# Layout of the scratch image planes and tokens in a four-layer image kernel on one Trainium2 core

## The chip, the cores and the metric

One core of a Trainium2 chip runs one launch of the whole program. The metric is the device time of that launch in microseconds (us). Everything is float32. The engines are PE (TensorE: matmuls and transposes), ACT (ScalarE), DVE (VectorE), POOL (GpSimd) and SP (SyncE, which here does nothing but issue DMAs and wait); 16 DMA engines move the data. Their mean busy share is called the DMA share below.

## The reference, cut to what matters

The input is an image of 256 x 256 pixels with 128 channels. Four layers follow one another, each a residual branch on a group-normed copy of the image: attention, a Fourier layer, a convolutional layer and a gated depthwise layer. The change touches the end of the third layer and the whole fourth:

```python
    # third layer, its last part: c2 is a matmul over channels at each pixel
    v = relu(c2(z)); p = concat([z[:, :, :1], z[:, :, 1:] + v[:, :, :-1]], axis=2)
    r = relu(c2(p)); q_main = r + roll(p, 1, axis=2)            # and the last two columns apart
    # fourth layer, T = 8 identical steps; the three 7x7 kernels are depthwise and circular
    gate_B = sigmoid(conv7x7(x, gate_B_kernel));  b_t = conv7x7(x, B_kernel) * gate_B
    a_t = A_kernel placed at the origin * sigmoid(conv7x7(x, gate_A_kernel))   # non-zero near the origin only
    log_h = heinsen_scan_log(...a_t, b_t, repeated T times...)
    out = x + exp(log_h[-1]) @ W_out + b_out
```

Away from the origin a_t is zero, so a pixel's result is a constant times (softplus(b_t) + 1e-6). A 7x7 patch at the origin is computed again in full at the end.

## The kernel before, in words

The stages run one after another, with a barrier of all engines between them. The last ones, in order, are `pointwise_part` (names begin with pw_), the group-norm coefficients, `patch_weights` (kw_), `depthwise_layer` (dw_) and `origin_patch` (og_). They pass data through three scratch tensors in DRAM.

`x3t[256 rows, 8 column offsets d, 32 patches, 128 ch]` is the third layer's result by tokens. `planes[33, 8 d, 8 y, 128 ch, 34]` is the same image by channels: the image is cut into patches of 8 x 8 pixels, and one cell (a channel's 34 numbers, 17,408 bytes for all channels) holds the pixels of one offset (y, d) of a row of patches, over all 32 patches and one wrapped patch on either side. Its rows are shifted by HALO = 3. `patch_w[32, 112, 2, 4, 128]` holds the depthwise taps spread into matmul weights.

`pointwise_part` steps over t, two image rows to a step, 128 steps plus 12 to drain. Per step SP loads two rows (L1374/L1376) and a broadcast row of tau (L1378) six steps ahead; DVE, PE, ACT and POOL pass them through z, v, p, r, q; DVE writes the result into `x3b` (L1520), which holds a band of 16 rows. Nine steps later PE turns the band's chunks (four patches each, eight chunks to a band) into `p_n` (L1450), and ACT copies each twice: into `x3n` (L1471), a double buffer that SP stores to x3t (L1389), and into `plane` (L1481). At the end of a band POOL fills the wrapped columns (L1423, L1424), and SP stores the whole band of `plane` at L1395 in three or four DMAs, one for each piece that `pieces(g)` finds. A piece is a run of n rows of one patch row; its DRAM side has the extents n x 8 x 4352, with n being 5, 8 and 3 in an inner band. SP's queue is in order, so the loads and token stores of the following steps stand behind these. ACT's L1471 waits at `tokens_stored` until the store of chunk e-2 has landed.

`patch_weights` makes 256 matmuls at 112 output rows (L1595) and stores patch_w in two DMAs (L1577).

`depthwise_layer` walks 8 blocks of 32 image rows. Its first half, per k (8 channels, 128 of them in all), loads windows (L1683, three DMAs: 24, 64 and 24 partitions, five patch rows, 1,080 bytes each) and twice 448 KB of weights (L1689), and PE does two `conv` (L1737, eight matmuls each, K = 112, the two halves being one patch row and the next). DVE and ACT copy the result into `raw`. Its second half, per unit u (128 of them), turns 8 pieces (L1749), ACT and DVE make gate, bt, soft and hid, PE projects (L1760), and DVE adds `xr`, the residual, into `outs` (L1880). The convs run 34 ahead (`lead`), so that k = u + 17. `xr` (L1695, 256 KB) is loaded in one DMA of 128 partitions, and `outs` is stored in four (L1702), one for each of four rows; the DRAM side of each has the extents 4 x 32 x 128, the SBUF side 128 x 128. All of it is issued by SP, which per unit does this:

```python
            for u in range(total + 8):
                k = u + lead // 2
                if k < BLOCKS * 16:
                    load_windows(k)      # waits for conv 2k-5
                    load_weights(2 * k)  # wait for conv 2k-4 and 2k-3
                    load_weights(2 * k + 1)
                if 0 <= u - 5 < total:
                    load_residual(u - 5)
                if 0 <= u - 8 < total:
                    store(u - 8)         # waits for added, then four DMAs
```

`origin_patch` loads a 13 x 13 patch of tokens in 27 short DMAs (L1943), and then computes the 49 pixels on one serial chain.

Of the kernel before, what the change touches and what calls it, by code (L numbers as in the profile page):

```python
# [1115 lines left out]
WIDE = PX + 2  # L1116
PATCH_ROWS = ROWS // PATCH + 1
# [183 lines left out]
def pointwise_part(nc, x2, tau, w2, b2, scale, shift, ident, x3t, planes, stats):  # L1301
# [6 lines left out]
    tokens = x3t.rearrange("(g y) d a c -> g (y d) (a c)", y=BAND)  # L1308
    with ExitStack() as ctx:
# [11 lines left out]
        x3b = m.sb("x3b", [128, 2, PX, BAND, PATCH])  # L1321
        x3n = m.sb("x3n", [128, 2, 4, CH])
# [8 lines left out]
        tokens_stored = [m.sem(f"tokens_stored{i}") for i in range(2)]  # L1331
# [3 lines left out]
        x3_made, counted, x3_turned = (m.sem(n) for n in ("x3_made", "counted", "x3_turned"))  # L1335
        tokens_read, plane_read, plane_wrapped = (m.sem(n) for n in ("tokens_read", "plane_read", "plane_wrapped"))
        block = ctx.enter_context(nc.Block())
        steps = range(-2, tiles + 12)

        def pieces(g):  # L1340

            first, found = g * BAND, []
            runs = [(y, min(y + BAND, ROWS), HALO) for y in (first,)]
            if g == 0:
                runs.append((0, PATCH - HALO, HALO + ROWS))
            if g == ROWS // BAND - 1:
                runs.append((ROWS - HALO, ROWS, HALO - ROWS))
            for start, stop, offset in runs:
                while start < stop:
                    at = start + offset  # L1350
                    n = min(stop - start, PATCH - at % PATCH)
                    found.append((start - first, n, at // PATCH, at % PATCH))
                    start += n
            return found

        def plane_stores(parity, g):

            return 16 * sum(len(pieces(k)) for k in range(parity, g, 2))

        @block.sync  # L1360
        def _(sp):
# [21 lines left out]
            for t in steps:  # L1383
# [3 lines left out]
                if 0 <= e < chunks:  # L1387
                    sp.wait_ge(tokens_read, e + 1)
                    sp.dma_start(tokens[e // 8][:, e % 8 * 4 * CH:(e % 8 + 1) * 4 * CH],  # L1389
                                 x3n[:, e % 2].rearrange("p a c -> p (a c)")).then_inc(tokens_stored[e % 2], 16)  # L1390
# [236 lines left out]
def depthwise_layer(nc, x3t, planes, patch_w, ksum, scale, shift, w_plain, b_plain, ident, out):  # L1627
# [11 lines left out]
    with ExitStack() as ctx:  # L1639
# [145 lines left out]
        def _(act):  # L1785
# [34 lines left out]
            for u in range(total + 2):  # L1820
# [3 lines left out]
                if 2 <= u:  # L1824
                    soft_first(u - 2)
# [345 lines left out]
```

## Time and profile before

| | |
|---|---|
| median of 3 runs | 7585.48 us (7583.73 to 7593.19) |
| the profiled execution's own time, and its span | 7594.39 us, 7592.7 us |
| mean granted TensorE clock over the span | 0.904 of full speed |
| PE, DVE, ACT, POOL busy | 6234.0 (82%), 3902.4 (51%), 3821.1 (50%), 569.5 us (8%) |
| moved by DMA | 773.64 MB, 102 GB/s over the span |
| matmuls of conv (L1737) | 643.6 us busy for x4096, and 412.5 us idle before them |
| ACT's first gate step (L1795) | 99.4 us busy, 792.2 us idle before it |

The page cuts the span in 40 slices of 190 us. Its rows of tenths show the busy share of each engine, of the DMA engines, and the clock that TensorE was granted:

```profile
PE   7999999999999999977999899854444557777763
PEclk9999999999999999999999999987777568888886
DMA  5111111111111111673111111355444189888882
```

Up to slice 26 attention and the Fourier layer run; `pointwise_part` fills slices 27 to 31, `patch_weights` the end of 31 and 32, and `depthwise_layer` the rest but for the last 66 us. SPq is SP's queue: its durations are the time that issuing the DMAs took. A matmul in float32 leaves two records, and its records overlap in time.

### The profile page before, as it was taken

What the parts mean: (1) busy time and instruction counts of PE and PEld (TensorE: products, weight loads), DVE (VectorE), ACT (ScalarE), POOL (GpSimd) and SP (SyncE); (2) the same over time, 40 slices, a digit from 0 to 9 for tenths busy, and PEclk for the clock granted to TensorE, in tenths of its full rate; (3) what the DMA queues carried; (4) which work ended last, traced back from release to release, by engine and by line L of the source; (5) the groups of instructions that cost most, each with busy time, mean ns of one, the idle gap of its engine ahead of it and who ended that gap; (6) DMA issues with size and microseconds to landing.
All of it is one profiled execution on the core that took longest, in us unless ns stands there. A gap on an engine that the chain in (4) does not pass through costs nothing. (4 is left out here: it accounts for less than half of the span.)

```text
span 7592.7 us, 110044 instructions
## 1 busy us (share of the span) xinstructions
PE 6234.0 (82%) x29856; PEld 4091.6 (54%) x29856; DVE 3902.4 (51%) x11300; ACT 3821.1 (50%) x9727; POOL 569.5 (8%) x879
## 2 busy tenths in 40 slices
PE   7999999999999999977999899854444557777763
PEld 5777777777777776424444344311111347766663
DVE  7777777777777777413333333224444203333335
ACT  3777777777777776223444444433333203333333
POOL 0000000000000000001000000013333000111111
PEclk9999999999999999999999999987777568888886
DMA  5111111111111111673111111355444189888882
GB/s 200 34 35 35 35 34 35 35 34 34 35 35 35 34 35 41 211 230 96 59 61 56 62 59 61 107 187 164 161 156 157 52 204 207 196 195 199 196 197 70
DMA packets 759166, 773.64 MB, mean 102 GB/s; under 512 B 52640, under 2 KB 631769, under 8 KB 748121
## 3 DMA queue, kind: packets, MB, share of 16 engines
q1 hardware_dynamic: 738986, 719.10, 33.9%
q0 software_dynamic: 13312, 41.96, 1.4%
q10 hardware_dynamic: 6720, 10.76, 0.4%
q8 instruction: 75, 1.23, 0.1%
q14 instruction: 73, 0.60, 0.0%
HBM read 566.01 MB, written 205.61 MB: 102 GB/s over the span
## 5 line engine op out<-in xcount | busy, mean ns | idle before, releaser
L428 ACT ACTIVATE at_probs<-at_neg_s,at_neg_max 128x256 f32<-128x256 f32 x2048 | 1018.0, 499 | 327.1 <-DVE at_neg_max L480 320.6
L359 PE MATMUL at_p_s<-at_keys,at_qz 128*128 128x256 f32 x4096 | 1107.0, 393 | 3.2 <-ACT at_qz L453 2.5
L480 DVE CUSTOM_DVE_ANT_0 at_neg_s<-at_p_s,at_bias 128x256 f32<-128x256 f32 x2048 | 782.2, 419 | 592.7 <-PE at_p_s L359 592.6
L1737 PE MATMUL dw_p_conv<-dw_xw,dw_wts 112*128 112x128 f32 x4096 | 643.6, 323 | 412.5 <-issue 349.1
L1737 PEld LDWEIGHTS dw_p_conv<-dw_xw,dw_wts 112*128 112x128 f32 x4096 | 609.8, 235 | 433.7 <-issue 432.9
L359 PEld LDWEIGHTS at_p_s<-at_keys,at_qz 128*128 128x128 f32 x4096 | 697.7, 190 | 267.4 <-issue 209.1
L347 PE MATMUL at_p_o<-at_probs_t,at_vs 128*32 128x256 f32 x4096 | 810.0, 385 | 0.0
L492 DVE TENSOR_SCALAR at_probs<-at_probs,at_inv 128x256 f32<-128x256 f32 x2048 | 631.0, 351 | 36.2
L339 PE MATMUL at_p_t<-all_ident,at_probs 128*128 128x128 f32 x4096 | 587.1, 276 | 1.6 <-DVE at_probs_t L471 1.6
L1443 PE MATMUL pw_p_r<-pw_p,pw_w 128*128 128x512 f32 x256 | 170.4, 753 | 459.8 <-DVE pw_p L1498 459.6
L339 PEld LDWEIGHTS at_p_t<-all_ident,at_probs 128*128 128x128 f32 x4096 | 466.8, 141 | 133.1 <-issue 105.9
L1795 ACT ACTIVATE dw_gate<-dw_p_turn,dw_f_shift,dw_nscale 128x512 f32<-128x512 f32 x128 | 99.4, 777 | 792.2 <-PE dw_p_turn L1749 792.2
L935 PE MATMUL ml_p<-ml_h,l_w 128*128 128x512 f32 x1024 | 485.0, 597 | 1.6 <-DVE ml_h L1002 1.6
L347 PEld LDWEIGHTS at_p_o<-at_probs_t,at_vs 128*32 128x32 f32 x4096 | 284.7, 109 | 368.2 <-issue 128.2
L951 PE MATMUL ml_p<-ml_h,l_w1s 128*128 128x512 f32 x1024 | 469.2, 601 | 1.3 <-DVE ml_normed L1010 1.3
L1872 DVE SCALAR_TENSOR_TENSOR dw_hid<-dw_bt,dw_soft 128x512 f32<-128x512 f32 x128 | 135.2, 1057 | 592.5 <-ACT dw_soft L1813 592.5
L422 ACT ACTIVATE at_probs_t<-at_p_t 128x512 f32<-128x512 f32 x512 | 305.9, 597 | 249.6 <-PE at_p_t L339 243.3
L453 ACT ACTIVATE at_qz<-at_p_qk 32x256 f32<-32x256 f32 x1024 | 384.3, 375 | 92.0 <-PE at_p_qk L405 82.9
L981 ACT ACTIVATE ml_h<-ml_p,l_b 128x512 f32<-128x512 f32 x384 | 248.0, 679 | 282.6 <-PE ml_p L935 282.6
L428 ACT ACTIVATION_READ_ACCUMULATOR at_probs<-at_neg_s,at_neg_max 128x1 f32 x2048 | 386.2, 189 | 0.0
L1443 PEld LDWEIGHTS pw_p_r<-pw_p,pw_w 128*128 128x128 f32 x256 | 49.0, 226 | 567.5 <-DVE pw_p L1498 547.0
L471 DVE COPY at_probs_t<-at_p_t 128x512 f32<-128x512 f32 x512 | 349.3, 682 | 0.5 <-PE at_p_t L339 0.5
(214 smaller groups left out, 9837.9 us busy)
## 6 DMA issues: line engine op xcount, KB each, us to landing
dw_wts<-patch_w SPq DMA_DIRECT2D x256, 448.0 KB, 8.2
sp_xs<-x SPq DMA_DIRECT2D x256, 256.0 KB, 3.2
dw_xw<-planes SPq DMA_DIRECT2D x128, 337.5 KB
in_xs<-in_x_dram SPq DMA_DIRECT2D x32, 1024.0 KB
at_xs<-in_x_dram SPq DMA_DIRECT2D x256, 128.0 KB, 2.1
at_kvs<-in_L_conv_kv_x_dram SPq DMA_DIRECT2D x256, 128.0 KB, 2.3
x<-at_x1s SPq DMA_DIRECT2D x256, 128.0 KB, 1.9
ml_xs<-x SPq DMA_DIRECT2D x128, 256.0 KB
```

The costliest lines, as they stand in the source:

```text
L339: mm = pe.transpose(p_t[h % 2][:, kh, qh * 128:(qh + 1) * 128], probs[:, h, qh, kh * 128:(kh + 1) * 128], ident[:, :])
L347: mm = pe.matmul(p_o[ch, 0, :], vs[:, row.r % 2, kh, ch], probs_t[:, h, kh, :], start=kh == 0, stop=kh == HALVES - 1)
L359: mm = pe.matmul(p_s[h % 2][:, qh, :], qz[:, row.r % 2, h, qh * 128:(qh + 1) * 128], keys[:, row.r, h // 2, :], start=True, stop=True)
L422: act.activation(probs_t[:, h], p_t[h % 2][:, :, :], ACT.Copy).then_inc(odd_read, 1)
L428: e = act.activation(probs[:, h, qh, :], neg_s[:, h % 2, qh, :], ACT.Exp, bias=neg_max[:, row.r % 2, i:i + 1], scale=-1.0, accum_out=sums[ ...
L453: t = act.activation(qz[ch, two.r % 2, h, :], p_qk[ch, 0, :], ACT.Copy, scale=float(HEAD_DIM) ** -0.5)
L471: dve.tensor_copy(probs_t[:, h], p_t[h % 2][:, :, :]).then_inc(even_read, 1)
L480: t = dve.tensor_tensor_reduce(neg_s[:, h % 2, qh, :], p_s[h % 2][:, qh, :], bias[:, h, qh, :], -1.0, 3.0e38, ALU.add, ALU.min, neg_max[:, ...
L492: t = dve.tensor_scalar(probs[:, h, qh, :], probs[:, h, qh, :], inv[:, p, j:j + 1], None, ALU.mult)
L935: pe.matmul(p_1[b][:, :], w0[:, b * 128:(b + 1) * 128], h[:, :], start=True, stop=True).then_inc(hid_made, 1)
L951: mm = pe.matmul(p_2[:, :], w1c[:, b, :], h1[:, b, :], start=b == 0, stop=b == blocks - 1)
L1737: mm = pe.matmul(p_conv[g % 2][:, j, :], wts[:, g % 4, half, j, :], xw[:, k % 3, half:half + BLOCK_PY, g % 2 * 4 + j, 0:PX], start=half == ...
```

## The change

The cells of `planes` become 16 rows x 8 columns on 128 partitions. A cell row is now an image row of 8 offsets, `planes[264, 8, 128 ch, 33]`, with the image shifted by SHIFT = 4 rows, and with 4 wrapped rows above and below. A conv window lies in two horizontally neighbouring cells, so that the two halves of a conv are the cell and the one to its right; a window load is one DMA of 128 partitions x 4 patch rows x 1,056 bytes. The weights take 128 rows rather than 112.

`x3t` becomes `[16 bands, 33 cells, 129, 128 ch]`. The tokens are shifted by 4 columns, and the 33rd cell wraps. `x3b` has 33 cells too; each DVE instruction of L1520 becomes two of half the size, and POOL copies the wrapped half cell once a band. PE and DVE wait for that.

The stores of `plane` go out in eight parts of 2,112 bytes on 128 partitions, one in each of the eight steps after the band, and the steps go on 20 beyond the last, not 12. POOL fills one wrapped column, not two. `x3n` has four buffers, and its stores are now pieces of 512 bytes rather than 2,048; every eighth step has one more, of 64 KB.

In `depthwise_layer` the residual comes in four DMAs of 32 partitions, one step later, and the result leaves in four of 32 partitions, x 4 rows x 512 bytes. ACT issues those at the end of its step, for unit u - 9, instead of SP. `xr` and `outs` have four buffers. `origin_patch` cuts its pieces at the cell edges too: about 53 loads rather than 27.

```diff
@@ pointwise_part
-        x3n = m.sb("x3n", [128, 2, 4, CH])
+        x3n = m.sb("x3n", [128, 4, 4, CH])
+        part = CH * WIDE // 8
@@ SP
-                if e >= 0 and e % 8 == 7:
-                    g = e // 8
-                    sp.wait_ge(plane_wrapped, g + 1)
-                    for y, n, r_at, y_at in pieces(g):
-                        sp.dma_start(planes[r_at, :, y_at:y_at + n].rearrange("d y c a -> y d (c a)"),
-                                     plane[y * PATCH:(y + n) * PATCH, g % 2].rearrange("p c a -> p (c a)")
-                                     ).then_inc(planes_stored[g % 2], 16)
+                f = t - 18
+                if 0 <= f < chunks:
+                    g, k = f // 8, f % 8
+                    flat = plane[:, g % 2].rearrange("p c a -> p (c a)")
+                    if k == 0:
+                        sp.wait_ge(plane_wrapped, g + 1)
+                    sp.dma_start(body[g][:, k * part:(k + 1) * part], flat[:, k * part:(k + 1) * part]
+                                 ).then_inc(planes_stored[g % 2], 16)
@@ PE, and the same for DVE's bn_stats
                     pe.wait_ge(x3_made, 8 * g + 8)
+                    pe.wait_ge(x3_wrapped, g + 1)
@@ DVE
                     for i in range(2):
-                        x3 = dve.scalar_tensor_tensor(out=x3b[:, g % 2, :, y + i, :],
+                        for d, a_at in ((0, 1), (SHIFT, 0)):
+                            cols = slice(SHIFT - d, 2 * SHIFT - d)
+                            x3 = dve.scalar_tensor_tensor(
+                                out=x3b[:, g % 2, a_at:a_at + PX, y + i, d:d + SHIFT],
@@ depthwise_layer
-        xw = m.sb("xw", [WROWS, 3, BLOCK_PY + 1, 8, WIDE])
+        xw = m.sb("xw", [128, 3, BLOCK_PY, 8, WIDE])
@@ SP
-                for d, n, at, col in ((PATCH - HALO, HALO, 0, 0), (0, PATCH, HALO, 1), (0, HALO, HALO + PATCH, 2)):
-                    sp.dma_start(flat[at * PATCH:(at + n) * PATCH, k % 3, :, 0:run],
-                                 field(b * BLOCK_PY, d, 0, c, col, n)).then_inc(x_loaded[k % 3], 16)
+                sp.dma_start(flat[:, k % 3], windows(b, c)).then_inc(x_loaded[k % 3], 16)
...
-            def store(w):
-                r, x, y = w // 4, w // 2 % 2 * 4, w % 2 * 4
-                sp.wait_ge(added, w + 1)
-                for i in range(4):
-                    sp.dma_start(out[0, r * PATCH + y + i].rearrange("(a d) c -> d a c", d=PATCH)[x:x + 4],
-                                 outs[:, w % 3, i]).then_inc(stored[w % 3], 16)
+                for d in range(4):
+                    sp.dma_start(xr[d * PX:(d + 1) * PX, w % 4], cells[(1 - x) * SHIFT + d][:, y:y + 4]).then_inc(r_loaded[w % 4], 16)
@@ PE
-                        mm = pe.matmul(p_conv[g % 2][:, j, :], wts[:, g % 4, half, j, :],
-                                       xw[:, k % 3, half:half + BLOCK_PY, g % 2 * 4 + j, 0:PX],
+                        mm = pe.matmul(p_conv[g % 2][:, j, :], wts[:, g % 4, side, j, :],
+                                       xw[:, k % 3, :, g % 2 * 4 + j, side:side + PX], start=side == 0, stop=side == 1)
@@ ACT
+            def store(w):
+                r, x, y = w // 4, w // 2 % 2 * 4, w % 2 * 4
+                act.wait_ge(added, w + 1)
+                for d in range(4):
+                    act.dma_start(out[0, r * PATCH + y:r * PATCH + y + 4].rearrange("y (a d) c -> d a y c", d=PATCH)[x + d],
+                                  outs[d * PX:(d + 1) * PX, w % 4]).then_inc(stored[w % 4], 16)
...
                 if u < total:
                     gate_third(u)
+                if 9 <= u:
+                    store(u - 9)
@@ origin_patch
-                k = min(left, 128 - at % 128)
+                k = min(left, 128 - at % 128, PATCH - (x + SHIFT) % PATCH)
```

## Rows read from the trace of the kernel before

**Rows 1.** SP's queue: start us, duration us; band stores of the pointwise stage and its end.
```profile
5154.59 6.18 SPq L1395 DMA_DIRECT2D planes<-pw_plane  x4
...
5214.35 3.78 SPq L1395 DMA_DIRECT2D planes<-pw_plane  x3
...
5944.77 6.01 SPq L1395 DMA_DIRECT2D planes<-pw_plane  x4
5981.09 0.35 SPq L1570 DMA_DIRECT2D all_taps<-in_L_conv_B_kernel_dram  x1
```

**Rows 2.** SP's queue around one band store, 5595 to 5624 us.
```profile
5595.83 3.77 SPq L1395 DMA_DIRECT2D planes<-pw_plane  x3
...
5612.19 3.14 SPq L1378 DMA_DIRECT2D pw_taus<-tau  x1
5623.70 0.32 SPq L1389 DMA_DIRECT2D x3t<-pw_x3n  x1
```

**Rows 3.** Who waited for whom, 5200 to 5700 us: total us, times, longest.
```profile
ACT pw_x3n L1471 <- DMA x3t<-pw_x3n: 224.6, 9, 25.2
```

**Rows 4.** Stretches: length, busy of PE, PEld, DVE, ACT, POOL; clock, DMA share, GB/s.
```profile
5122.00:5150.00 28.00, 20.18 (x63) 9.01 (x63) 23.37 (x36) 17.09 (x31) 17.07 (x31) 0.94 0.69 216
5560.00:5569.00 9.00, 0.00 (x0) 0.00 (x0) 0.00 (x0) 0.00 (x0) 0.00 (x0) 0.50 0.26 93
6112.00:6150.00 38.00, 0.00 (x0) 0.00 (x0) 0.00 (x0) 0.00 (x0) 0.00 (x0) 0.50 0.86 285
6200.00:6260.00 60.00, 43.43 (x271) 41.91 (x270) 6.08 (x9) 5.38 (x9) 0.00 (x0) 0.76 1.03 221
6400.00:7300.00 900.00, 640.37 (x4138) 626.50 (x4139) 306.94 (x431) 296.77 (x520) 110.03 (x86) 0.83 0.85 197
7404.00:7500.00 96.00, 63.45 (x334) 61.57 (x335) 57.72 (x75) 52.75 (x90) 24.60 (x19) 0.71 0.36 104
```

**Rows 5.** Groups by line, 5122 to 5150 us: shapes xcount | busy us, mean ns | idle before.
```profile
L1520 DVE SCALAR_TENSOR_TENSOR pw_x3b<-pw_xs,all_coef,pw_q 128x256 f32<-128x256 f32 x14 | 6.2, 481 | 4.5 <-POOL pw_q L1418 4.3
```

**Rows 6.** DVE in order of time: two instructions of L1511, eight steps apart.
```profile
5121.77 1.67 DVE L1511 SCALAR_TENSOR_TENSOR pw_z<-pw_xs,all_coef,pw_taus 128x512 f32<-128x512 f32 x1
...
5152.85 0.74 DVE L1511 SCALAR_TENSOR_TENSOR pw_z<-pw_xs,all_coef,pw_taus 128x512 f32<-128x512 f32 x1
```

**Rows 7.** SP's queue: first window load, the 18th and the last of 128.
```profile
6154.36 1.66 SPq L1683 DMA_DIRECT2D dw_xw<-planes  x3
...
6266.93 1.65 SPq L1683 DMA_DIRECT2D dw_xw<-planes  x3
...
7394.44 1.98 SPq L1683 DMA_DIRECT2D dw_xw<-planes  x3
```

**Rows 8.** SP's queue in one unit of the depthwise stage.
```profile
6804.65 0.38 SPq L1695 DMA_DIRECT2D dw_xr<-x3t  x1
6805.07 5.52 SPq L1702 DMA_DIRECT2D out_dram<-dw_outs  x4
6810.64 1.90 SPq L1683 DMA_DIRECT2D dw_xw<-planes  x3
6812.59 0.83 SPq L1689 DMA_DIRECT2D dw_wts<-patch_w  x2
```

**Rows 9.** PE in order of time through one unit.
```profile
6809.72 2.02 PE L1737 MATMUL dw_p_conv<-dw_xw,dw_wts 112*128 112x128 f32 x16 [2.04 <-issue]
6811.58 1.05 PE L1760 MATMUL dw_p_out<-all_w_plain,dw_hid 128*128 128x128 f32 x8
6812.47 1.96 PE L1737 MATMUL dw_p_conv<-dw_xw,dw_wts 112*128 112x128 f32 x16
6814.26 1.33 PE L1749 MATMUL dw_p_turn<-all_ident,dw_raw 128*128 128x128 f32 x8
```

**Rows 10.** ACT's queue, a store of the Fourier layer.
```profile
3211.72 0.32 ACTq L641 DMA_DIRECT2D spec<-sp_out  x1
```
**Rows 11.** SP's queue, the loads of the origin patch.
```profile
7527.34 9.02 SPq L1943 DMA_DIRECT2D og_xs<-x3t  x27
```

More of the change, by code:

```diff
@@ L1330, in pointwise_part @@
         wrap_loaded = m.sem("wrap_loaded")
-        tokens_stored = [m.sem(f"tokens_stored{i}") for i in range(2)]
+        tokens_stored = [m.sem(f"tokens_stored{i}") for i in range(4)]
         planes_stored = [m.sem(f"planes_stored{i}") for i in range(2)]
@@ L1334, in pointwise_part, with token_stores @@
         r_mul, r_made, p_wrapped, q_made = (m.sem(n) for n in ("r_mul", "r_made", "p_wrapped", "q_made"))
-        x3_made, counted, x3_turned = (m.sem(n) for n in ("x3_made", "counted", "x3_turned"))
+        x3_made, x3_wrapped, counted, x3_turned = (m.sem(n) for n in ("x3_made", "x3_wrapped", "counted", "x3_turned"))
         tokens_read, plane_read, plane_wrapped = (m.sem(n) for n in ("tokens_read", "plane_read", "plane_wrapped"))
         block = ctx.enter_context(nc.Block())
[L1338 to L1354, printed above, removed]
+        steps = range(-2, tiles + 20)
+        bands = ROWS // BAND
+        edge = SHIFT * PATCH
+        first_row = planes[0:SHIFT].rearrange("y d c a -> (y d) (c a)")
+        last_row = planes[ROWS + SHIFT:ROWS + 2 * SHIFT].rearrange("y d c a -> (y d) (c a)")
+        body = planes[SHIFT:ROWS + SHIFT].rearrange("(g y) d c a -> g (y d) (c a)", y=BAND)
+        part = CH * WIDE // 8
+        def token_stores(e):
+            return 16 * (e // 4) + (16 * len(range(0, e, 8)) if e % 4 == 0 else 0)
         def plane_stores(parity, g):
-            return 16 * sum(len(pieces(k)) for k in range(parity, g, 2))
+            return 16 * 8 * len(range(parity, g, 2)) + (16 if parity == 0 and g > 0 else 0) + (16 if g == bands and parity else 0)
         @block.sync
@@ L1559, in patch_weights @@
         p_t = m.ps("p_t", [KTAPS, 2, CH])
-        p_w = [m.ps(f"p_w{i}", [WROWS, 2, 2, CH]) for i in range(4)]
+        p_w = [m.ps(f"p_w{i}", [128, 2, 2, CH]) for i in range(4)]
         p_b = m.ps("p_b", [128, CH])
@@ L1658, in depthwise_layer @@
         w_loaded = [m.sem(f"w_loaded{i}") for i in range(4)]
-        r_loaded = [m.sem(f"r_loaded{i}") for i in range(3)]
-        stored = [m.sem(f"stored{i}") for i in range(3)]
+        r_loaded = [m.sem(f"r_loaded{i}") for i in range(4)]
+        stored = [m.sem(f"stored{i}") for i in range(4)]
         scaled, prepared, biased = m.sem("scaled"), m.sem("prepared"), m.sem("biased")
@@ L1712, in _ @@
                 load_weights(2 * k + 1)
-            for u in range(total + 8):
+            for u in range(total + 6):
                 k = u + lead // 2
@@ L1718, in _ @@
                     load_weights(2 * k + 1)
-                if 0 <= u - 5 < total:
-                    load_residual(u - 5)
-                if 0 <= u - 8 < total:
-                    store(u - 8)
-            for s in range(3):
-                sp.wait_ge(stored[s], 64 * ((total - s + 2) // 3))
+                if 0 <= u - 6 < total:
+                    load_residual(u - 6)
         @block.tensor
@@ L1833, in _ @@
                     gate_third(u)
+                if 9 <= u:
+                    store(u - 9)
+            for s in range(4):
+                act.wait_ge(stored[s], 64 * (total // 4))
         @block.gpsimd
@@ L1877, in residual @@
                 dve.wait_ge(biased, w + 1)
[L1878 to L1880 removed]
+                if w >= 4:
+                    dve.wait_ge(stored[w % 4], 64 * (w // 4))
+                dve.tensor_tensor(outs[:, w % 4], p_out[w % 2][:, :, :], xr[:, w % 4], ALU.add).then_inc(added, 1)
             for g in range(0, lead, 2):
@@ L1937, in origin_patch, with cells @@
         loads = len(pieces) + 4 + 2 * SIDE
+        def cells(y, x, k):
+            first = y % BAND * PATCH + x % PATCH
+            return x3t[y // BAND, x // PATCH, first:first + k]
         @block.sync
```

114 lines of the change are left out of this document (58 added, 56 removed).

## The prediction

> **What bounds the kernel now.** Only the last 2500 us or so are touched, so I read the page's slices first and then go by stages. In slices 27 to 31 and from 33 on PE is not full, and the DMA share is either low (4 or 5 tenths) or high (8). These are two different limits.
>
> *The pointwise stage.* The stores of a band go out at 5154.59, 5214.35 and so on, the last of 16 at 5944.77, and the next stage begins at 5981.09 [rows 1]. The 15 bands between take 790 us, 52.7 each, or 6.6 us a step. But the first band, when no planes are yet being stored, runs at 31.08 us for eight steps, 3.89 each [rows 6]. So nearly half of the stage is something else. SP's queue shows it: the band's store is issued at 5595.83, everything behind it takes 1 to 3 us to issue, and the next token store gets out at 5623.70 only [rows 2]. ACT stands at L1471 for a token store to land, 224.6 us in 500, 25 us at a time [rows 3]. What is in flight then is seen in the stretches: at 5560 to 5569 no engine works, and the 16 DMA engines are 0.26 busy at 93 GB/s [rows 4]. A share of 0.26 over engines that have work queued means that about 4 of 16 do it. The stores of plane are cut along an outer extent of 5, 8 and 3, and those of patch_w, whose outer extent is 112, reach 0.86 at 285 GB/s [rows 4]. I read this as: a store is spread over as many engines as its outer extent allows.
>
> The Trainium skill, "DMA: Bandwidth & Descriptors", section on why a DMA increments its semaphore by 16, says that a copy runs on the largest number up to 16 that divides both sides' slowest extents. By it 5, 8 and 3 engines work for plane, a mean of 4 to 5 of 16, and the share of 0.26 agrees; it also gives 4 for the result's stores, below.
>
> *The depthwise stage.* 110 units pass between the 18th window load at 6266.93 and the last at 7394.44: 10.25 us each [rows 7]. PE needs about 6.36 us of them (2.02 + 1.05 + 1.96 + 1.33) and waits before conv for nothing an engine did ("issue"), that is, for a load [rows 9]. DVE and ACT work 307 and 297 us in 900, or 86 units: 3.6 and 3.4 us a unit [rows 4]. The DMA share is 0.85 at 197 GB/s. But SP has no idle time: the four result stores take 5.52 us to issue, windows 1.90, weights 0.83, the residual 0.38 [rows 8]. One residual load carries as much as all four stores and takes a fourteenth of the time to issue, so the stores are held back by full queues, on the few engines that they reach, and the loads that PE waits for stand behind them.
>
> **What the DMA engines can do.** I divide GB/s by share in each stretch of [rows 4]: 216/0.69 = 313 in the pointwise stage's clean band, 285/0.86 = 331 for patch_w, 104/0.36 = 289 in the depthwise tail (512-byte pieces only); but 221/1.03 = 215 in the depthwise lead (windows and weights on 112 partitions, no stores), and 197/0.85 = 232 in its steady part. That the lead is so slow at 4,096- and 1,080-byte pieces is the open point: either it is the uneven 24-, 64- and 24-partition loads and the 112 rows, which go, or the source layout, which stays. Bounds for the new stage: 232 and 331.
>
> **The change part by part.**
> 1. *Plane stores in eight even parts.* The stall goes. What is late next is the step's own loop: 3.89 us [rows 6]. L1520 becomes four instructions of half the size. One of 256 elements takes 481 ns [rows 5]; one of 128 takes between half of that and all of it, so a step gains 0 to 0.96 us. With a fixed part of about 0.2 us I take 0.25: 4.13 a step. POOL's wrap is one small copy a band and the waits on it fall a step before they are needed: nothing; were it late, a POOL copy is under 0.7 us a band (10 us in all). From the first band store, moved to 5159, 110 steps to the last image step come to 454 us (5613), the ten drain steps to about 2 us each (5633). The end, now 36 us, shrinks: 2.2 MB at 93 GB/s take 24 us, at 313 GB/s 7, so 19 are left. End at 5652 instead of 5981: 329 gained. ACT's wait for the plane buffer at a band's first chunk now comes in the same step in which the last part is issued; up to 2 us a band, of which I count 9 in all. **−320** (bounds −230, all of 0.96 a step, and −350). The DMA load of a step is four transfers of about 262 KB, 1.07 MB in 4.13 us, 260 GB/s, which is under 313: near the limit, but not at it.
> 2. *patch_w* grows from 14.7 to 16.8 MB; its store runs at 285 GB/s: 0 to +7, **+4**.
> 3. *Lead of the depthwise stage.* 17 k in 112.6 us, 6.62 each [rows 7]. Now 541 KB of windows and 1,049 of weights (before 605 and 918). At 313 GB/s 5.1 us, which is above the two convs' 4.0: **−26** (at 215: +13).
> 4. *A unit of the steady part.* Bytes: 541 + 1,049 + 262 of residual + 262 of result = 2,114 KB, 3% more than before. Windows and weights at 313 give 5.1 us, the 512-byte transfers at 289 1.8, together 6.9. PE needs 6.36, SP now 0.6 + 0.83 + 4 x 0.4 = 3.0, ACT 3.4 + 4 x 0.4 (issues of 0.32 [rows 10] with gaps) = 5.1 in busy time. Nothing has slack to spare, so 6.9 won't be met wholly: **7.2 us**, 110 x (10.25 − 7.2) = **−336**. Bounds: PE's 6.4 (−423) and 2,114 KB at 232 GB/s, 9.1 (−127). I take the fast side because 313, 289 and 331 are three stretches with evenly spread transfers, and 215 and 232 the two without.
> 5. *ACT's stores.* Behind them on ACT stands the next gate step, which PE's turns two units on and, through DVE's copy, the next conv wait for. They wait for `added` of unit u − 9, which DVE made two steps before: no wait. The tail of 17 units (7404 to 7500: ACT 52.75 of 96 busy [rows 4]) may lose what the issues cost ACT, and gains SP's: nothing. The last stores spread: **−5**.
> 6. *Origin patch.* 27 loads take 9.02 us to issue [rows 11]; 26 more at 0.334 on the serial path: **+9**.
>
> Sum: −320 + 4 − 26 − 336 − 5 + 9 = −674. From the profiled execution's 7594.4: 6920; it lies 8.9 above the median of the runs, so **6910** for the median.
>
> **The rivals.**
> - *A faster case* is inside the forecast's own range: 6.4 us a unit gives 6820.
> - *B. The rate stays.* The loads run at 215 to 232 because of the cells' pitch in DRAM or of the mixture. Then a unit is 9.2 us and the lead 7.4: 6910 + 220 + 39 = 7170. For it: the share of 1.03 in the lead with no store in sight [rows 4]. Against it: the clean stretches.
> - *C. 32 partitions.* Residual and result now touch 32 partitions at a time. If that halves the tail's rate, to 145 GB/s, they cost 3.6 us instead of 1.8, and a unit about 8.8: +176, 7085. The tail, with 128 partitions, cannot show it. The Trainium skill, "SBUF — State Buffer", section on the DMA port swizzle, says that partitions 0 to 31 reach 8 of 16 ports, 189 GB/s at 1 MiB; by it the two cost an estimated 2.8 us, and the sum would be 110 higher. No row here tests it.
> - *D. The jam moves to ACT.* If the four stores still take 5.5 us to issue, ACT needs 3.9 (its six instructions end to end) + 5.5 = 9.4 a unit: 7150. The skill's DMA page, "Issuing engines are not separate DMA queues", says that another issuer saves its own issue time only; that the present hold-up lies in few engines speaks against D.
> - *E. The pointwise stall stays,* because the parts are not spread as I think, or because 512-byte token stores replace it by a DMA limit: some 260 of the 320 are lost, 7170.
> - *F. Slower than before.* D with a worse price: ACT's issues block so long that the gate chain runs late each unit. It decides from 674/110 + 7.2 = 13.3 us a unit, that is 9.4 us for four issues, against 5.52 now; at 11 us a unit takes 14.9 and the time is 7760.
>
> **How the numbers follow.** Chances: forecast 0.58, B 0.14, C 0.12, D 0.08, E 0.06, F 0.02. The forecast's own range, from its bounds without B's rate, is 6790 to 7030. Eight in ten reach from 6780 to 7180, which takes in B to D as priced. A difference of under 0.2% could not be told from none. All but F are faster by far more: faster 0.97, within 0.2% 0.01, slower 0.02.
>
> **What would show it.** Pointwise: band stores about 33 us apart, ACT's wait for token stores gone, DMA share 0.7 to 0.85, and the stage's end about 320 us earlier. If bands take 38 us or more, DVE's four instructions or the DMA rate were mis-sized. Depthwise: window loads 7.2 us apart, GB/s around 290 in the steady part, SP idle for over half, the 512-byte stores on ACT's queue 1.3 to 1.7 us a group, PE's granted clock up from 0.83 as it waits less. B would show as a share near 1 at under 235 GB/s, in the lead too; C as a normal lead and a slow steady part; D as store groups over 4 us on ACT's queue.

## The result: 6768 us, and the profile after

The changed kernel takes 6768.24 us (median of 4 runs, 6760.24 to 6776.89); its ratio to the kernel before is 0.892 (95% interval 0.8904 to 0.8935). The kernel before, with a fourth run, has a median of 7588.18 us. That is faster by 820 us, where 674 were forecast, and 12 us below the lower end of the range. The profiled execution has a span of 6766.9 us against 7592.7.

The stages can be cut at the same instructions of SP's queue in both traces: the first load of each stage, the 18th window load, the last window load.

| stage | before, us | after, us | change | forecast |
|---|---|---|---|---|
| up to the pointwise stage | 5077.3 | 5078.1 | +0.8 | 0 |
| pointwise, with the coefficients | 903.8 | 557.3 | −346.4 | −320 |
| patch_weights | 173.3 | 165.0 | −8.2 | +4 |
| depthwise, lead (17 k) | 112.6 | 70.5 | −42.0 | −26 |
| depthwise, 110 units | 1127.5 | 704.5 | −423.0 | −336 |
| depthwise, tail | 132.9 | 118.6 | −14.3 | −5 |
| origin patch | 65.4 | 72.9 | +7.5 | +9 |

The cuts are rows like these, of SP's queue in the changed kernel (start us, duration us); they answer to [rows 1, 7 and 11]:

```profile
5635.42 0.34 SPq L1577 DMA_DIRECT2D all_taps<-in_L_conv_B_kernel_dram  x1
...
5800.45 0.36 SPq L1688 DMA_DIRECT2D dw_xw<-planes  x1
...
5870.98 0.93 SPq L1688 DMA_DIRECT2D dw_xw<-planes  x1
...
6575.46 0.44 SPq L1688 DMA_DIRECT2D dw_xw<-planes  x1
...
6694.03 16.40 SPq L1952 DMA_DIRECT2D og_xs<-x3t  x53
```

The same kernel's stretches, with the columns of [rows 4] (length, busy of PE, PEld, DVE, ACT and POOL, granted clock, DMA share, GB/s): the pointwise stage after its first bands, the store of patch_w, the lead, the steady part and the tail.

```profile
5157.00:5558.00 401.00, 277.51 (x794) 121.08 (x793) 357.31 (x696) 228.06 (x397) 232.38 (x425) 0.92 0.90 270
5765.00:5795.00 30.00, 0.00 (x0) 0.00 (x0) 0.00 (x0) 0.00 (x0) 0.00 (x0) 0.50 1.03 386
5815.00:5865.00 50.00, 45.32 (x385) 43.54 (x384) 8.15 (x13) 7.17 (x12) 0.00 (x0) 1.00 1.03 377
5950.00:6500.00 550.00, 500.36 (x4087) 486.39 (x4087) 297.09 (x424) 291.86 (x510) 114.79 (x85) 1.00 1.09 328
6600.00:6670.00 70.00, 44.89 (x245) 42.16 (x243) 47.36 (x60) 43.58 (x74) 21.07 (x15) 0.78 0.43 115
```

Three things are to be seen beside [rows 4]. In the steady part PE is 91% busy at a granted clock of 1.00 (before: 71% at 0.83), the DMA engines move 328 GB/s instead of 197, and they are full (share 1.09; it sums the times of packets and passes 1 where these overlap). In the lead, with no store in sight in either kernel, the rate went from 221 to 377 GB/s at the same share of 1.03. And in the pointwise stage DVE is busy 357 of 401 us.

One number from such a row is used for every run below. A unit leaves 48 matmul records (32 of conv, 8 of turn, 8 of project), so a stretch's length over its PE count, times 48, is the time of a unit: 550/4087 x 48 = 6.46 us here, 900/4138 x 48 = 10.44 us in [rows 4]. (The table's 704.5/110 gives 6.40, since the first units are quicker.)

PE's order of time through one unit in the changed kernel, as in [rows 9]:

```profile
6304.15 2.02 PE L1731 MATMUL dw_p_conv<-dw_xw,dw_wts 128*128 128x128 f32 x16 [0.69 <-issue]
6306.01 1.06 PE L1753 MATMUL dw_p_out<-all_w_plain,dw_hid 128*128 128x128 f32 x8
6306.91 1.95 PE L1731 MATMUL dw_p_conv<-dw_xw,dw_wts 128*128 128x128 f32 x16
6308.69 1.33 PE L1742 MATMUL dw_p_turn<-all_ident,dw_raw 128*128 128x128 f32 x8
6310.65 2.02 PE L1731 MATMUL dw_p_conv<-dw_xw,dw_wts 128*128 128x128 f32 x16 [0.62 <-issue]
```

From 6304.15 to 6310.65 is 6.50 us. The four groups add up to 6.36, but their records overlap at the joints, so that PE works 5.88 and waits 0.62, before the first conv only. The 6.36 that the prediction took as PE's least was too much by this overlap.

### The profile page after: what moved, and what is told of

Its sections match the earlier page's. It is cut to its first block and busy times, and to the rows that moved or that the text cites. A ratio compares the mean times of both kernels' runs of the same rounds, so it can differ in the third digit from the quotient of the medians.

```text
span 6766.9 us, 110680 instructions
## 1 busy us (share of the span) xinstructions
PE 6039.0 (89%) x29856; PEld 3899.9 (58%) x29856; DVE 3958.6 (58%) x11556; ACT 3822.8 (56%) x9727; POOL 587.2 (9%) x879
## 5 line engine op out<-in xcount | busy, mean ns | idle before, releaser
L1731 PE MATMUL dw_p_conv<-dw_xw,dw_wts 128*128 128x128 f32 x4096 | 509.5, 277 | 122.5 <-issue 64.3
L1731 PEld LDWEIGHTS dw_p_conv<-dw_xw,dw_wts 128*128 128x128 f32 x4096 | 479.7, 190 | 142.7 <-issue 141.0
L935 PEld LDWEIGHTS ml_p<-ml_h,l_w 128*128 128x128 f32 x1024 | 195.7, 191 | 250.7 <-issue 246.0
L1010 DVE SCALAR_TENSOR_TENSOR ml_normed<-ml_p,l_vec,ml_rstd 128x512 f32<-128x512 f32 x128 | 96.1, 751 | 410.6 <-ACT ml_rstd L975 410.6
L707 POOL DMA_DIRECT2D mixed<-mx_gs x64 | 34.8, 545 | 3350.3 <-DVE mx_gs L767 3345.8
```

The source lines that it names most:

```text
L935: pe.matmul(p_1[b][:, :], w0[:, b * 128:(b + 1) * 128], h[:, :], start=True, stop=True).then_inc(hid_made, 1)
L1731: mm = pe.matmul(p_conv[g % 2][:, j, :], wts[:, g % 4, side, j, :], xw[:, k % 3, :, g % 2 * 4 + j, side:side + PX], start=side == 0, stop= ...
```

## The experiments

Theory 1 is the prediction's: how a transfer is cut decides how fast it drains, and SP's queue passes a slow one's price on to all that stands behind it. Theory 2, its main rival, is the other half of the change: what counts is that loads and stores shared one queue. A third question came with the result: why loads alone, in the lead, are 1.7 times as fast. Times are of one run where no interval is given; they are compared with 7588 (before) and 6768 (after).

### The result's stores: their cut and their queue

Four runs cross the two halves. In the kernel before, the even cut alone:

```diff
-                for i in range(4):
-                    sp.dma_start(out[0, r * PATCH + y + i].rearrange("(a d) c -> d a c", d=PATCH)[x:x + 4],
-                                 outs[:, w % 3, i]).then_inc(stored[w % 3], 16)
+                for d in range(4):
+                    sp.dma_start(out[0, r * PATCH + y:r * PATCH + y + 4].rearrange("y (a d) c -> d a y c", d=PATCH)[x + d],
+                                 outs[d * PX:(d + 1) * PX, w % 3]).then_inc(stored[w % 3], 16)
```

> The kernel before, with one edit: the result's four stores of a unit are cut as in the changed kernel (32 partitions x 4 rows of 512 bytes each, DRAM side 32 x 4 x 128), still issued by SP from the same place; the data and the bytes are the same. Theory 1 (a store reaches only as many DMA engines as its outer extents allow, and the old cut reached few): the group of four issues falls from 5.5 us to about 2, PE's next limit is the rate of windows and weights, 1522 KB at 221 GB/s plus 524 KB at 289 GB/s = 8.7 us a unit instead of 10.25, total about 7415 us (7380 to 7480). Theory 2 (what matters is that SP's queue issues loads and stores in turn, whatever their cut): the unit stays at 10.25 us and the total at 7588, within 20.

Measured: 7409.4 us, theory 1's number (7415) and far from theory 2's. A unit takes 800/4387 x 48 = 8.75 us, as the sum of bytes over rates had given (8.7). The new limit is plain in the steady stretch of this run: the DMA share is 1.02 at only 235 GB/s, against 0.85 and 197 in [rows 4].

```profile
6400.00:7200.00 800.00, 624.52 (x4387) 610.78 (x4388) 334.88 (x458) 313.74 (x550) 124.40 (x92) 0.88 1.02 235
```

Then ACT's queue alone, with the old cut:

```diff
-                if 0 <= u - 8 < total:
-                    store(u - 8)         # SP
+                if 9 <= u:
+                    store(u - 9)         # ACT, after gate_third(u)
```

> The kernel before, with one edit: the result's stores keep their old cut (four DMAs of 128 partitions, DRAM side 4 x 32 x 128) but ACT issues them, for unit u-9, and SP's queue has loads alone. Theory 1: the few engines that carry the stores stay the slowest, so the hold-up moves to ACT's queue (groups of about 5 us there) and a unit stays at 9.5 us or more, total 7500 to 7650. Theory 2: SP's queue is free, a unit falls to 7 or 8 us, total 7250 to 7350.

Measured: 7495.6 us, 4 us below theory 1's range and 145 above theory 2's; a unit takes 800/4064 x 48 = 9.45 us. The hold-up is now on ACT's queue, and the next gate step (L1785) waits behind it:

```profile
6810.59 0.55 ACTq L1812 DMA_DIRECT2D out_dram<-dw_outs  x1
6810.93 0.62 ACT L1803 ACTIVATE dw_soft<-dw_soft 128x512 f32<-128x512 f32 x1
6811.45 0.71 ACT L1794 ACTIVATE dw_gate<-dw_gate,dw_log_scale 128x512 f32<-128x512 f32 x1
6811.46 6.65 ACTq L1812 DMA_DIRECT2D out_dram<-dw_outs  x3
6818.25 0.78 ACT L1785 ACTIVATE dw_gate<-dw_p_turn,dw_f_shift,dw_nscale 128x512 f32<-128x512 f32 x1 [6.09 <-PE dw_p_turn L1739]
```

This is the prediction's rival D, made to happen. It shows that the queue is worth something too: 93 us while the cut is uneven. In the changed kernel the old cut was put back, ACT still issuing (the first diff in reverse):

> The changed kernel, with one part undone: the result's stores are cut as before (four DMAs of 128 partitions, DRAM side 4 x 32 x 128, one image row each), but ACT still issues them; which partitions hold which pixels is the same in both cuts, so the result is too. Theory 1: the engines that they reach carry 66 KB more than the others, a unit rises from 6.5 to 8 us or more, total 6930 or more. Theory 2: the cut doesn't matter, total 6768 within 20.

Measured: 6982.8 us, 215 more; a unit takes 550/3099 x 48 = 8.52 us, at a DMA share of 0.90 and 248 GB/s. Theory 1 again, which had asked for 8 us or more and 6930 or more. Last, the new cut, issued by SP again:

```diff
+                if 0 <= u - 8 < total:
+                    store(u - 8)         # SP, behind load_residual(u - 6)
-                if 9 <= u:
-                    store(u - 9)         # ACT
```

> The changed kernel, with one part undone: the result's stores, in their new even cut, are issued by SP again, for unit u-8 behind the residual's loads. Theory 1: SP needs 0.5 + 1 + 1.9 + 1.7 = 5 us of the 6.5 us of a unit, nothing is late, total within 30 us of the changed kernel's 6768. Theory 2: loads wait behind stores again, at least 1 us a unit, total 6880 or more.

Measured: 6859.5 us (ratio to before 0.9035, 0.902 to 0.905), 91 more than the changed kernel. Both expectations missed: mine of at most 30, and theory 2's of 112 or more. SP had time enough to issue (its four stores take 1.76 us). It was the wait in front of them, in this run's list of who waited for whom from 5950 to 6500 us:

```profile
SPq L1715 <- DVE dw_outs L1884: 100.1, 59, 3.8
```

SP's loads run two units ahead of PE, and `store(u - 8)` makes it wait for a sum that DVE has yet to make. If so, an older unit's store waits for nothing:

```diff
-                if 0 <= u - 8 < total:
-                    store(u - 8)
+                if 0 <= u - 10 < total:
+                    store(u - 10)
```

> The changed kernel with the stores of the result issued by SP in the even cut, as in the run that lost 91 us, but two units later (u-10 instead of u-8). In that run SP waited at the store for DVE's sum, 100 us in 550, with the next loads behind it. If that wait is what ACT's queue saves, it is gone here, and the total is 6768 within 15. If the issuing itself costs (SP's queue shared by loads and stores), at least 40 us of the 91 stay.

Measured: 6756.1 us (ratio 0.8905, 0.8891 to 0.8919), all of the 91 us back and 12 more. A unit takes 450/3362 x 48 = 6.42 us. So ACT's queue as such gives nothing: it spares SP a wait, and so does a store two units later. Whether the 12 us beyond are real is taken up below.

### Why loads alone became faster

Each load of weights in the changed kernel was split in two, first at partition 112 and then at 64 as its control:

```diff
-                sp.dma_start(wts[:, g % 4], patch_w[g % groups]).then_inc(w_loaded[g % 4], 16)
+                for lo, hi in ((0, 112), (112, 128)):      # in the other run (0, 64), (64, 128)
+                    sp.dma_start(wts[lo:hi, g % 4], patch_w[g % groups][lo:hi]).then_inc(w_loaded[g % 4], 16)
```

> The changed kernel, with one edit: each load of weights is two DMAs, of partitions 0 to 111 and 112 to 127; bytes are the same. It asks why the lead of the depthwise stage runs at 370 GB/s where it ran at 221 before. If loads onto 112 partitions are slow by themselves, most of the difference comes back: lead under 290 GB/s, a unit of the steady part over 7 us, total over 6830. If it was the three uneven window loads or the source's layout, nothing comes back but for the issues: total under 6800.

> The changed kernel, with one edit: each load of weights is two DMAs of 64 partitions. The control for the 112-partition edit: two DMAs as there, but on even numbers of rows per engine. If the 112 are the cause there, this one is nearer to the changed kernel (370 GB/s in the lead, total under 6800), unless half the partitions at a time are slower by themselves; if two DMAs instead of one are the cause, both lose alike.

Measured: 6992.8 and 6989.4 us, and units of 8.05 and 8.31 us. The lead's rate, in the stretch of 377 GB/s above, in the run at 112 and the run at 64:

```profile
5815.00:5865.00 50.00, 30.74 (x231) 28.88 (x231) 4.84 (x7) 4.78 (x8) 0.00 (x0) 0.95 1.07 251
```

```profile
5815.00:5865.00 50.00, 31.29 (x239) 29.03 (x238) 5.53 (x8) 4.18 (x7) 0.00 (x0) 0.97 1.07 249
```

The same bytes, the same share, two thirds of the rate. But both lose alike, so it isn't the odd number 112. Either any load that doesn't span the 128 partitions is slow, or two DMAs are. The same split in two along the free side tells:

```diff
+                for side in range(2):
+                    sp.dma_start(wts[:, g % 4, side], patch_w[g % groups][:, side]).then_inc(w_loaded[g % 4], 16)
```

> The changed kernel, with one edit: each load of weights is two DMAs of all 128 partitions, 2,048 bytes each (the two sides apart). The control that the runs with 112 + 16 and 64 + 64 partitions left open: they fell from 377 to about 250 GB/s in the lead alike. If that was because no DMA of theirs spans the 128 partitions, this one stays near the changed kernel: lead over 340 GB/s, total under 6810. If it was because there are twice as many DMAs, this one falls as they did: lead near 250 GB/s, total about 6990.

Measured: 6769.7 us, a lead at 359 GB/s, a unit of 450/3288 x 48 = 6.57 us. As many DMAs as in the two runs before, and nothing is lost in the total. So what costs is the cut along the partitions, and not the number of DMAs.

The Trainium skill, "SBUF — State Buffer", section on the DMA port swizzle, says that only a transfer over all 128 partitions reaches all 16 ports at once and that 0 to 63 reach no more than 0 to 31; the run at 64 agrees (249 GB/s against 377 and 359). The run at 112 is as slow (251), and there the port count explains less: by the same section's table, 0 to 111 touch all 16 ports, unevenly. Whether its part of 112 or its rest of 16 partitions is the slow one was not tried.

From the other side: the kernel before with 16 rows of zeros added to the weights.

```diff
-    patch_w = scratch("patch_w", [CH // 4, WROWS, 2, 4, 2 * SPOTS])
+    patch_w = scratch("patch_w", [CH // 4, 128, 2, 4, 2 * SPOTS])
-        wts = m.sb("wts", [WROWS, 4, 2, 4, 2 * SPOTS])
+        wts = m.sb("wts", [128, 4, 2, 4, 2 * SPOTS])
```

> The kernel before, with one edit: the scratch weights have 128 rows, of which the last 16 are zeros, and the weights' loads and the store of patch_w span the 128 partitions; the convs still use 112 rows. If the span of 128 partitions is what makes loads fast, weights land faster though they have 14% more bytes: the lead's rate rises from 221 GB/s, at least to 270, and its 18 window loads take under 100 us instead of 113. The steady part is held by the stores on few engines and stays near 10.25 us a unit; total 7540 to 7590. If the layout of the source is the cause, the lead gets longer by the bytes, 118 us or more.

Measured: 7494.6 us, 94 less than before, for 14% more bytes of weights. The store of patch_w, whose partitions are the one thing about it that changed, now runs at the changed kernel's rate; before, it had a share of 0.86 and 285 GB/s [rows 4]:

```profile
6115.00:6145.00 30.00, 0.00 (x0) 0.00 (x0) 0.00 (x0) 0.00 (x0) 0.00 (x0) 0.50 1.03 384
```

The lead did not follow. From its first window load (6159.92) to the 18th (6272.23) it takes 112.3 us, against 112.6 before: neither the 100 of the one explanation nor the 118 of the other. Its rate from 6200 to 6250 us is 218 GB/s. So whole weights alone don't make the lead fast. What this lead lacks against the changed kernel's 70.5 us lies with the windows, the only load in it that still differs: three DMAs of 24, 64 and 24 partitions and five patch rows became one of 128 partitions and four. An estimate from these runs: at 377 GB/s the 1,049 KB of weights take 2.8 of this run's 6.6 us a k, and the rest leaves 158 GB/s for 605 KB of windows. Whether the windows were slow by their cut or by their layout in DRAM no run separates. The steady part, which I had expected unchanged, went to 800/4162 x 48 = 9.23 us a unit. Why it gained what the lead didn't is open.

### What sets a unit of 6.5 us now

The rest is PE's 5.88 us of work and 0.62 of waiting. Half of the weights' bytes were left out, with all waits kept:

```diff
-                sp.dma_start(wts[:, g % 4], patch_w[g % groups]).then_inc(w_loaded[g % 4], 16)
+                sides = slice(0, 2) if g < 4 else slice(0, 1)
+                sp.dma_start(wts[:, g % 4, sides], patch_w[g % groups][:, sides]).then_inc(w_loaded[g % 4], 16)
```

> The changed kernel, leaving out a part: from the fifth group on only the weights of one side are loaded, 256 KB instead of 512 KB; the convs use old data for the other side. PE's work and every wait are as before. It asks what sets the 6.50 us of a unit, in which PE works 5.88 and waits 0.62 before the first conv. If it is the DMA engines (share 1.09), a unit falls to 5.9 us, total about 6700. If it is the chain of turn, gates, copy and conv over ACT and DVE, or the granted clock, the unit stays at 6.5 and the total within 15 of 6768, but for the lead.

Measured: 6675.3 us, and PE has no gap left in its groups by line from 5950 to 6400 us (shapes xcount | busy us, mean ns | idle before):

```profile
L1732 PE MATMUL dw_p_conv<-dw_xw,dw_wts 128*128 128x128 f32 x2529 | 311.3, 274 | 0.0
L1743 PE MATMUL dw_p_turn<-all_ident,dw_raw 128*128 128x128 f32 x639 | 106.8, 310 | 0.0
L1754 PE MATMUL dw_p_out<-all_w_plain,dw_hid 128*128 128x128 f32 x632 | 83.8, 276 | 0.0
```

A unit takes 450/3800 x 48 = 5.68 us. With fewer bytes the DMA engines' hold on the unit is gone and PE is busy throughout. So the changed kernel's units are bound by the DMA engines, as the prediction said, at 328 GB/s, and PE is only 0.8 us behind.

### The plane stores

In the kernel before, a band's stores were issued row by row:

```diff
-                        sp.dma_start(planes[r_at, :, y_at:y_at + n].rearrange("d y c a -> y d (c a)"),
-                                     plane[y * PATCH:(y + n) * PATCH, g % 2].rearrange("p c a -> p (c a)")
+                        for i in range(n):
+                            sp.dma_start(planes[r_at, :, y_at + i].rearrange("d c a -> d (c a)"),
+                                         plane[(y + i) * PATCH:(y + i + 1) * PATCH, g % 2].rearrange("p c a -> p (c a)")
```

> The kernel before, with one edit: the stores of a band of plane go out one image row at a time (16 or more DMAs of 8 partitions x 17,408 bytes) instead of in pieces of 5, 8 and 3 rows; the bytes are the same, and so is the place in SP's queue. If a store is spread by its outer extent, each now reaches 8 engines instead of 5, 8 and 3: the 2.2 MB drain in about half the time, the DMA share in the stall is near 0.5 instead of 0.26, and the band's period falls from 54 us to 42 to 46 (stage 120 to 190 us shorter, total about 7430). Rival (the stall is the write rate of these long pieces in DRAM, or their place in the queue): period 54 us as before, total 7588 within 20.

Measured: 7597.8 us. The time is the rival's, and of the theory only the share came true. In the stall, where the kernel before had a share of 0.26 and 93 GB/s [rows 4]:

```profile
5560.00:5569.00 9.00, 0.00 (x0) 0.00 (x0) 0.00 (x0) 0.00 (x0) 0.00 (x0) 0.57 0.50 114
```

Twice the share, and a quarter more bytes a second; SP takes 19.83 us to issue the band's 16 DMAs. More engines are not the remedy by themselves. Why they moved so little each, this run doesn't show. The opposite edit in the changed kernel kept the old pieces, which there have one merged extent:

```diff
-                    sp.dma_start(body[g][:, k * part:(k + 1) * part], flat[:, k * part:(k + 1) * part]
-                                 ).then_inc(planes_stored[g % 2], 16)
+                        for lo, hi in ((0, 40), (40, 104), (104, 128)):   # all at k == 0
+                            sp.dma_start(body[g][lo:hi], flat[lo:hi]).then_inc(planes_stored[g % 2], 16)
```

> The changed kernel, with one edit: a band of plane goes out in three DMAs of 40, 64 and 24 partitions x 16,896 bytes, the pieces of the kernel before, but with (row, offset) as one outer extent of 40, 64 and 24, since the new cells lie in that order. If the old extents of 5, 8 and 3 were the cause, these are spread over 8 engines or more, and the stage is within 60 us of the changed kernel's 557. If a store has to span the 128 partitions to be fast, the drain stays near 120 GB/s, ACT waits for token stores at each band again, and the stage is 200 us longer or more (about 760 or more).

Measured: 6782.1 us; the stage, from its first load at 5079.89 to the next stage's at 5653.04, takes 573 us against 557. ACT's waits for a token store, 224.6 us in 500 before [rows 3], come to this in 401 us:

```profile
ACT pw_x3n L1476 <- DMA x3t<-pw_x3n: 26.0, 12, 4.4
```

In the changed kernel there is no such wait in this stretch. While the three pieces of a band drain, with the step's other transfers, the engines move nearly three times what they did in the stall before:

```profile
5421.00:5431.00 10.00, 5.64 (x17) 2.46 (x18) 9.70 (x18) 5.57 (x10) 6.90 (x11) 1.00 0.84 273
```

So the stores of plane need not span the 128 partitions, nor be cut in eight: three whole pieces do nearly as well in the new layout. What in it does this is not separated. The outer extent is now 40, 64 or 24 and not 5, 8 or 3; but a piece is now also one unbroken run in DRAM, where two neighbouring offsets of a row used to lie 139 KB apart, and x3n has four buffers instead of two. And all eight parts at once:

```diff
-                    sp.dma_start(body[g][:, k * part:(k + 1) * part], flat[:, k * part:(k + 1) * part]
+                        for h in range(8):                                # all at k == 0
+                            sp.dma_start(body[g][:, h * part:(h + 1) * part], flat[:, h * part:(h + 1) * part]
```

> The changed kernel, with one part undone: the eight even parts of a band of plane are all issued in one step, not one a step. If the gain in the pointwise stage is from the even cut, the burst of 2.2 MB takes 7 us at over 300 GB/s, of which loads six steps ahead hide nearly all: the stage is within 30 us of the changed kernel's 557, total under 6800. If it is from the spreading over time, ACT and the loads stall at each band again by 5 us or more: stage 80 us longer, total 6850.

Measured: 6777.5 us, the stage 551 us (5083.16 to 5634.51). Spreading the parts over the steps gives nothing that one run can show.

### A version that beats both

The price of the new layout is 26 more short loads in the last stage. They can be shared with ACT:

```diff
-            for at, y, x, k in pieces:
+            for at, y, x, k in pieces[0::2]:          # SP; ACT issues pieces[1::2] and the residual's 14
```

> The changed kernel, with one edit: in the last stage half of the 53 token loads and all 14 loads of the residual are issued by ACT, which is idle there, while SP issues the rest. The 16.4 us of SP's issues become about 8.5, and the residual's 4.4 run beside them: total 8 to 13 us less, 6757. If the last loads' landing or ACT's table load behind the issues sets the end instead, less than 5 us.

Measured: 6755.2 us (ratio 0.8902, 0.889 to 0.8914). The stage takes 63.3 us instead of 72.9. Both queues run side by side:

```profile
6698.66 8.45 SPq L1952 DMA_DIRECT2D og_xs<-x3t  x27
6698.67 8.25 ACTq L1981 DMA_DIRECT2D og_xs<-x3t  x26
```

With the late stores from SP, and beside the changed kernel itself on the same chip:

> The changed kernel with two edits that were run alone: the result's stores issued by SP two units late, and the last stage's short loads shared between SP and ACT. They touch different stages, so the gains should add: 12 and 13 us below the changed kernel's 6768, that is 6743 (6735 to 6752). If the 12 us of the late stores are the difference between chips, 6755.

> The changed kernel itself, unedited, on the chip of the version above, to compare the two at equal terms. 6768 within 10.

Measured: 6751.2 us (6742.66 to 6755.77; ratio to before 0.8893, 0.888 to 0.8905) against 6771.3 (6758.99 to 6773.35; 0.8919, 0.8906 to 0.8932). It is 20 us, or 0.3%, faster than the changed kernel; of these the last stage gives 9.7 (72.8 to 63.1 us in the two traces) and the depthwise stage 5.1 (895.9 to 890.8). The two edits gave less together than the 25 expected. Which of them was worth less than it seemed is open: the runs of each edit alone and these two sets all come from one chip, so it was not a difference between chips, and the runs of one kernel lie up to 17 us apart.

## Why the prediction was wrong, point by point

**What bounds the kernel** was right in both stages: b_even_stores came within 6 us of a number worked out from it, and the pointwise stall went with the new stores. The reading that a store is spread over as many engines as its outer extent allows is borne out in the share (0.50 for an extent of 8), though loosely in the stall itself: 5, 8 and 3 have a mean of 5.3 engines, a share of 0.33, where 0.26 was seen. But the prediction took it for the whole cause of the slow drain, and b_row_stores shows that it isn't: the share doubled and the time stayed. What else the new layout does for these stores is open.

**The step that failed is "What the DMA engines can do".** It set 331 GB/s at full share as the upper bound, from the store of patch_w. That store itself ran on 112 partitions, and so was slowed by the very thing that the change removes: on 128 it runs at 386 GB/s, share 1.03, and at 384 in the kernel before with nothing but the 16 rows added (b_w128). The lead runs at 377, not 313. The text named the uneven loads and the 112 rows as one of two explanations of the slow 215 and took the fast side, but then priced it from the stretches of before, none of which had whole-partition loads of 4,096 bytes in it. (b_w128 shows that the weights' 112 rows alone were not what held the lead; the windows remain.) Every term on that rate was too small:
- the lead: 4.1 us a k instead of 5.1, −42 instead of −26;
- patch_weights: −8 instead of +4, at 14% more bytes;
- a unit: 6.40 instead of 7.2, which is −423 instead of −336. The lower bound of the text was PE's 6.4, and the measured value sits on it; that is a coincidence, for PE's least is 5.7 (a_half_weights), and the unit is bound by DMA at 328 GB/s where the sum had 2,114 KB at 306 and then a surcharge of 0.3 us. The surcharge had the reason that nothing has slack. It wasn't needed, and makes 33 of the 87 us: while DMA was full, PE's granted clock rose to 1.00 and its wait fell to 0.62 us.

**The pointwise stage** went as forecast, with the stall gone, and was mis-sized by 26 us. The extra band stores (the 33rd cell's, one a band) are 31.98 us apart, 4.00 a step instead of 4.13:

```profile
5189.48 0.51 SPq L1385 DMA_DIRECT2D x3t<-pw_x3n  x1
...
5349.37 0.50 SPq L1385 DMA_DIRECT2D x3t<-pw_x3n  x1
```

The four half instructions take 1.15 us of DVE's busy time a step (106.2 for 368, in the group below), against 0.89 for the two before (6.2 for 14 [rows 5]): 0.27 more, near the 0.25 taken. ACT's wait for the plane buffer, priced at 9 us with a bound of 2 us a band, is 19.1 in 12 waits. This is the changed kernel's DVE group of the line, from 5190 to 5560 us:

```profile
L1527 DVE SCALAR_TENSOR_TENSOR pw_x3b<-pw_xs,all_coef,pw_q 128x128 f32<-128x128 f32 x368 | 106.2, 350 | 40.7 <-POOL pw_q L1419 37.8
```

And this is the wait, from the list of who waited for whom, 5150 to 5560 us:

```profile
ACT pw_plane L1486 <- DMA planes<-pw_plane: 19.1, 12, 3.1
```

DVE is now the busiest engine of the stage, with 357 of 401 us; whether it is all that bounds it was not tried.

**ACT's stores.** I priced the four issues at 1.6 us on top of ACT's own work. They cost it next to nothing:

```profile
6303.51 0.78 ACT L1788 ACTIVATE dw_gate<-dw_p_turn,dw_f_shift,dw_nscale 128x512 f32<-128x512 f32 x1 [3.04 <-PE dw_p_turn L1742]
...
6305.36 0.32 ACTq L1815 DMA_DIRECT2D out_dram<-dw_outs  x1
6305.70 0.62 ACT L1806 ACTIVATE dw_soft<-dw_soft 128x512 f32<-128x512 f32 x1
6305.72 0.95 ACTq L1815 DMA_DIRECT2D out_dram<-dw_outs  x2
6306.22 0.71 ACT L1797 ACTIVATE dw_gate<-dw_gate,dw_log_scale 128x512 f32<-128x512 f32 x1
6306.69 0.49 ACTq L1815 DMA_DIRECT2D out_dram<-dw_outs  x1
```

The issues run beside the activations that were queued before them: the last issue ends at 6307.18, the last activation at 6306.93, and ACT then waits 3.1 us for PE. The wait that they do save, SP's on `added`, stood in the prediction only as no wait for ACT; that the same store on SP would cost 91 us (a_sp_stores) I had not seen.

**The rivals.** B (the rate stays) fell with the lead's 377 GB/s, and a_w112, with a lead at 251 GB/s, shows what a rate near B's costs: 225 us. C (32 partitions at a time) is there but small: the tail runs at 115/0.43 = 267 GB/s for a full share against 289 before, 8% less and not half, and the 110 us more that the prediction estimated are not seen in units of 6.40. (Its own price for C, 8.8 us a unit, should have been 9.0: 7.2 + 1.8.) D and F didn't come, as the cut was even; b_act_stores and a_uneven_stores show D's mechanism. E is refuted by the stage's 557 us.

**The range** held every rival on the slow side. On the fast side only two terms had a bound, the pointwise stage (−350) and the unit (6.4 us), and the measured −346 and 6.40 just keep to them. What carried the time out of the range were the three that had none, the lead, patch_weights and the tail: 16 + 12 + 9 us.

## What to carry to other kernels

A transfer's cut can be worth as much as its bytes: here the same bytes ran at 377 GB/s on all 128 partitions and at 250 in two parts of them, and the result's stores, cut evenly, gave 179 us in the kernel before. When DMAs seem to bound a stage, divide GB/s by share in several stretches, and ask of each stretch whether it has the fault that the change removes before taking it as a bound. A store that stands in a queue before loads has to be late enough never to wait; then the queue it stands in matters little.

## What the runs showed of the hardware that was not expected

- Splitting each load of weights in two along the partitions cost a third of the lead's rate (377 to 251 and 249 GB/s at a share of 1.07); splitting it along the free side cost 5% (359).
- The same store to DRAM ran at 285 GB/s from 112 partitions and at 384 from 128 (b_w128).
- Stores of 8 partitions each doubled the DMA share of the drain (0.26 to 0.50) and gave 114 GB/s instead of 93. A high share is no sign of a high rate.
- DMA issues on ACT's queue run beside its activations: four issues, 1.8 us in sum, within 3.7 us in which ACT also ran six activations.
